# Lookup layer of an eight-layer token kernel: the first pair sum of each tile waits for the tile's candidate sums

## The chip, the core and the metric

The kernel runs on one core of a Trainium2 chip. A core has five engines that run their own instruction streams in order: PE (TensorE, matrix products and transposes), DVE (VectorE), ACT (ScalarE), POOL (GpSimd) and SP (SyncE, which issues transfers here). They are ordered against each other by semaphores: an instruction waits until a counter has reached a value, and adds to a counter when it is done. The metric is the device time of one launch in microseconds (us). For the kernel before, three timed runs took 1604.61, 1605.89 and 1609.22 us; their median is 1605.89 us.

## The reference, cut to what matters

The program takes 2048 tokens (8 x 256) of width 128 through four attention layers and four feed-forward layers in turn. The change lies in the second feed-forward layer, a lookup in a table by product keys:

```python
q = (xn @ w_q.T).reshape(b, s, 2, NH, KD).transpose(2, 0, 1, 3, 4)
sim = jnp.einsum('pbnhd,hkpd->pbnhk', q, keys_p)          # 2 x 8 heads x 32 keys
scores, idx = jax.lax.top_k(sim, K)                       # the best 8 of 32, twice
all_scores = scores[0][..., :, None] + scores[1][..., None, :]
sc, pk = jax.lax.top_k(all_scores, K)                     # the best 8 of the 64 sums
...
hmid = jnp.einsum('bnd,bnhkd->bnhk', inputs, down[indices])
hmid = jax.nn.sigmoid(sc) * jax.nn.gelu(hmid, approximate=False)
return jnp.einsum('bnhk,bnhkd->bnd', hmid, up[indices])
```

For each token and each of 8 heads, two lists of 32 similarities are added pairwise (1024 sums). The eight largest sums name eight table rows, and each of these rows counts with the sigmoid of its sum.

## The kernel before

The whole layer works on tiles of 128 tokens, of which there are 16. Nothing is gathered: all 1024 pair sums of a head are formed, and those below the eighth best are masked to zero. One tile goes through the engines like this (the line numbers are those of the listing and of the profile):

- PE forms the similarities of the tile (L1653), and ACT copies them from PSUM to `sims` (tile `sb_OT`, L1730, semaphore `sims_ready`).
- POOL forms, head by head, the 1024 **pair sums** into a ring of four slots, `pairsum` (tile `sb_KM`, L1773, semaphore `sum_ready`). From the fifth sum of the layer on, a sum waits until its slot has been read (`gated_ready`, L1771): sum 0 of a tile waits for head 4 of the tile before, sum 1 for head 5, and so on.
- DVE finds in the meantime the threshold of each head. **tops** takes 16 times the best 8 of 32 (L1805). **combine** adds the 20 pairs of these that can be among the best 8, in four tensor-tensor additions for all heads at once (L1812, from `sb_top` to `sb_QT`, semaphore `combos_done`, which grows by four a tile). **bests** takes the best 8 of the 20 for each head (L1822).
- ACT takes the sigmoid of each head's pair sums (L1748, into PSUM). Two PSUM halves take turns, so that the sigmoid of head h waits for head h-2 to be masked.
- DVE **masks** head by head (L1846): a sigmoid stays where the pair sum is at or above the eighth best, and becomes zero elsewhere. The result goes to `gated` (tile `sb_both`, semaphore `gated_ready`).
- PE turns each masked head and adds the eight heads up (L1677). DVE multiplies by the GELU of the products with the table (**mix**, L1831). PE multiplies with the second table (**upper**, L1667), and DVE adds the tile to the residual (**add**, L1836).
- PE forms the products with the first table for the next tile (**lower**, two halves, L1658), and ACT takes their GELU (L1738). ACT has to load another function table before the GELUs and again before the next sigmoid (rows ACT_TABLE_LOAD, of L1738 and L1748).

Heads 0 to 7 of a tile follow each other on DVE in one stream, and the work for the next tile is put between them by hand:

```python
        def step(first, last_, i, t):
            ...
            for h in range(PK_HEADS):
                ...                                   # mask head h (L1846)
                if h == 0 and first > 0:
                    mix(i - 1, t - 1)
                if h == 4:
                    if first > 0:
                        add_tile(i - 1)
                    if last_ > 0:
                        tops(i + 1, t + 1, 0, 16)
                        combine(i + 1, t + 1)
                if h == 5 and last_ > 0:
                    bests(i + 1, t + 1, 0, 4)
```

So the tops and the combine of tile i+1 stand on DVE between the masks of heads 4 and 5 of tile i. ACT's stream has the two GELUs of tile i+1 between the sigmoids of heads 6 and 7 of tile i. The first four tiles and the last four are written out; the eight between them run in a loop over four tiles (L1619 to L1629). Transfers play no part in this layer.

Of the kernel before, what the change touches and what calls it, by code (L numbers as in the profile page):

```python
# [1340 lines left out]
BANDS = ((0, 1, 8, 0), (1, 2, 4, 8), (2, 4, 2, 12), (4, 8, 1, 16))  # L1341
# [5 lines left out]
def feed_forward(nc, ctx, sb, sem, S, w):  # L1347
# [75 lines left out]
    top_done, combos_done, best_done = sem("top_done"), sem("combos_done"), sem("best_done")  # L1423
# [195 lines left out]
    def steps1(eng, step):  # L1619


        far = TILES
        for t in range(TPG):
            step(t, far, t, t)
        with eng.Fori(1, GROUPS - 1) as g:
            for t in range(TPG):
                step(far, far, TPG * g + t, t)
        for t in range(TPG):
            step(far, TPG - 1 - t, TILES - TPG + t, t)  # L1629
# [134 lines left out]
    def pool1(pool, A):  # L1764
        def step(first, last_, i, t):

            pool.wait_ge(sims_ready, i + 1)
            s = sims[:, t % 4, :].rearrange("p (h q k) -> p h q k", h=PK_HEADS, q=2)
            for h in range(PK_HEADS):
                if first > 0 or h >= 4:  # L1770
                    pool.wait_ge(gated_ready, PK_HEADS * i + h - 3)  # L1771
                dst = pairsum[:, h % 4, :].rearrange("p (i j) -> p i j", i=NK)
                pool.tensor_tensor(dst, s[:, h, 0, :].unsqueeze(2).broadcast_to([P, NK, NK]),  # L1773
                                   s[:, h, 1, :].unsqueeze(1).broadcast_to([P, NK, NK]), ALU.add)\
                    .then_inc(sum_ready, 1)

        steps1(pool, step)
# [616 lines left out]
```

## Time and profile before

| what | value |
|---|---|
| median of three timed runs | 1605.89 us (1604.61 to 1609.22) |
| the profiled execution's own time | 1600.34 us |
| its span, from the first to the last instruction | 1598.5 us |
| busy in the span: PE, DVE, ACT, POOL | 1406.6, 1023.4, 909.5, 706.3 us |
| mean granted clock of TensorE | 0.956 |
| the layer of the change, in the span | from 544 to 819 us, 275 us |
| POOL's 128 pair sums (L1773) | 240.2 us busy, 1912 ns each |
| DVE's 128 masks (L1846) | 158.4 us busy, 1274 ns each |
| ACT's 128 sigmoids (L1748) | 129.6 us busy, 1023 ns each |

Times in the rows are microseconds from the start of the span. A busy share over the whole span says little about this layer: PE is the busiest engine of the program, but the layer has its own order of work, and POOL, DVE and ACT hand it to each other tile by tile. It is read from the timeline of one tile, and then from how the tiles differ. Durations of POOL's instructions are rough in a profile; the distance between two starts is the better measure of one sum.

### The profile page before, as it was taken

How to read it: one execution, taken by the hardware profiler on the slowest of the kernel's cores; microseconds unless marked ns; L12 is line 12 of the kernel's file. 1: busy time of each engine (PE TensorE's matmuls, PEld its weight loads, DVE VectorE, ACT ScalarE, POOL GpSimd, SP SyncE). 2: the span in 40 equal slices, each digit the busy share in tenths (PEclk: the TensorE clock that was granted, in tenths of full speed). 3: DMA queues.
4: the chain of work that ended last, by engine and by line, in shares of the span. 5: the costliest groups of instructions: out<-in, count | busy, mean ns of one | idle time of the engine just before them, and what ended most of it. 6: DMA issues, size and time to landing. Idle time of an engine off the chain costs nothing.

```text
span 1598.5 us, 30106 instructions
## 1 busy us (share of the span) xinstructions
PE 1406.6 (88%) x9483; PEld 945.5 (59%) x9497; DVE 1023.4 (64%) x3372; ACT 909.5 (57%) x1883; POOL 706.3 (44%) x1068
## 2 busy tenths in 40 slices
PE   5997789999998577887778987799899999998998
PEld 2544357777776466776754553444477777775543
DVE  5663467666775799999965553443476666765444
ACT  3665356666665477777746664423376666664321
POOL 5341144554453589989854330100164444542300
PEclk9999799999999599999899999799999999998999
DMA  2007000000000000000000000000000000000000
GB/s 68 18 21 287 1 5 7 3 3 3 3 3 1 27 1 1 1 0 0 1 1 1 1 1 1 27 1 0 3 5 4 3 3 3 3 1 1 1 14 13
DMA packets 12666, 21.78 MB, mean 14 GB/s; under 512 B 3088, under 2 KB 9120, under 8 KB 11936
## 3 DMA queue, kind: packets, MB, share of 16 engines
q1 hardware_dynamic: 12576, 20.63, 3.7%
q8 instruction: 50, 0.82, 0.2%
q14 instruction: 40, 0.33, 0.1%
HBM read 19.58 MB, written 1.05 MB: 13 GB/s over the span
## 4 chain that ended last, share of the span: by engine, by line
PE 68%; DVE 15%; ACT 9%; issue 6%; POOL 1%; DVEq 0%; DMA 0%; ACTq 0%; SPq 0%; POOLq 0%
PE bank L934 7%; PE bank L969 7%; PE bank L947 6%; DVE sb_both L1846 4%; PE bank L900 4%; PE bank L921 4%; PE bank L1879 3%; PE bank L2118 3%; PE bank L901 3%; PE bank L913 3%; PE bank L409 2%; PE bank L451 2%; ACT sb_KM L598 2%; ACT sb_both L598 2%; ACT bank L1748 2%
## 5 line engine op out<-in xcount | busy, mean ns | idle before, releaser
L1213 POOL TENSOR_TENSOR sb_both<-sb_both,sb_winv 128x512 f32<-128x512 f32 x256 | 260.9, 1040 | 292.4 <-DVE sb_winv L1143 292.4
L1036 ACT ACTIVATE sb_both<-sb_both,sb_wneg 128x256 f32<-128x256 f32 x512 | 253.0, 495 | 126.8 <-DVE sb_wneg L1137 126.8
L1773 POOL TENSOR_TENSOR sb_KM<-sb_OT 128x1024 f32<-128x1024 f32 x128 | 240.2, 1912 | 31.9 <-DVE sb_both L1846 27.9
L1677 PE MATMUL bank<-sb_ident,sb_both 128*128 128x128 f32 x1024 | 139.2, 286 | 60.8 <-DVE sb_both L1846 38.6
L1137 DVE CUSTOM_DVE_ANT_0 sb_both<-bank,sb_pen 128x256 f32<-128x256 f32 x512 | 182.1, 420 | 0.0
L1296 POOL TENSOR_TENSOR sb_ntmp<-sb_rstd 128x2 f32<-128x2 f32 (+2 forms) x123 | 24.1, 196 | 338.5 <-DVE sb_rstd L218 332.1
L1846 DVE SCALAR_TENSOR_TENSOR sb_both<-sb_KM,sb_best,bank 128x1024 f32<-128x1024 f32 x128 | 158.4, 1274 | 10.6 <-ACT bank L1748 10.4
L1677 PEld LDWEIGHTS bank<-sb_ident,sb_both 128*128 128x128 f32 x1024 | 118.8, 147 | 75.3 <-DVE sb_both L1846 48.9
L1748 ACT ACTIVATE bank<-sb_KM 128x1024 f32<-128x1024 f32 x128 | 129.6, 1023 | 36.4 <-DVE sb_both L1846 31.9
L947 PE MATMUL bank<-sb_ident,sb_both 128*128 128x128 f32 x1024 | 134.1, 273 | 8.7 <-DVE sb_QT L1150 5.9
L947 PEld LDWEIGHTS bank<-sb_ident,sb_both 128*128 128x128 f32 x1024 | 118.3, 141 | 27.2 <-issue 12.7
L934 PE MATMUL bank<-sb_KM 64*128 64x256 f32 x1024 | 127.8, 389 | 0.0
L969 PE MATMUL bank<-sb_QT,sb_VP 128*64 128x256 f32 x1024 | 124.6, 385 | 3.2 <-DVE sb_QT L1150 1.6
L1150 DVE COPY sb_QT<-bank 128x512 f32<-128x512 f32 x128 | 88.0, 687 | 39.8 <-PE bank L947 39.0
L934 PEld LDWEIGHTS bank<-sb_KM 64*128 64x128 f32 x1024 | 93.5, 186 | 19.3 <-issue 7.7
L969 PEld LDWEIGHTS bank<-sb_QT,sb_VP 128*64 128x64 f32 x1024 | 68.6, 136 | 50.9 <-issue 21.9
L1036 ACT ACTIVATION_READ_ACCUMULATOR sb_both<-sb_both,sb_wneg 128x1 f32 x512 | 95.8, 187 | 0.0
L1046 ACT ACTIVATE sb_QT<-bank 128x512 f32<-128x512 f32 x128 | 75.1, 587 | 29.2 <-PE bank L947 29.2
L692 DVE TENSOR_REDUCE sb_VP<-bank 128x4 f32<-128x1024 f32 (+1 forms) x48 | 58.7, 1224 | 37.0 <-PE bank L415 36.8
L583 ACT ACTIVATE sb_xnT_all<-bank 128x1024 f32<-128x1024 f32 x48 | 49.0, 1022 | 52.7 <-PE bank L415 52.7
L1027 ACT ACTIVATE sb_KM<-bank 128x512 f32<-128x512 f32 x64 | 38.2, 597 | 58.2 <-PE bank L901 58.1
L1107 DVE COPY sb_KM<-bank 128x512 f32<-128x512 f32 x64 | 44.1, 690 | 39.8 <-PE bank L901 39.8
(282 smaller groups left out, 2769.3 us busy)
## 6 DMA issues: line engine op xcount, KB each, us to landing
sb_ctxT_in<-in_ctxT SPq DMA_DIRECT2D x24, 128.0 KB, 2.3
sb_F<-in_F SPq DMA_DIRECT2D x2, 1024.0 KB
sb_XO<-in_ctx SPq DMA_DIRECT2D x8, 128.0 KB, 2.0
sb_WKQ<-in_WKQ SPq DMA_DIRECT2D x1, 1024.0 KB, 9.0
sb_W1ALL<-in_ctxT SPq DMA_DIRECT2D x1, 1024.0 KB, 4.9
sb_xn_all<-in_keymask SPq DMA_DIRECT2D x1, 1024.0 KB, 4.5
out_x<-sb_x SPq DMA_DIRECT2D x4, 256.0 KB, 2.3
sb_x<-in_x SPq DMA_DIRECT2D x1, 896.0 KB, 5.0
```

Source lines behind the costliest of these rows:

```text
L934: last = pe.matmul(s[:, h, i, :], QK[rows, t, 0, i * P:(i + 1) * P], QK[rows, t, 1, :], start=True, stop=True)
L947: last = pe.transpose(bank[4 + i][:, n * P:(n + 1) * P], PRW[:, t % 4, h, i, kt * P:(kt + 1) * P], ident[:])
L969: last = pe.matmul(bank[6][rows, (t % 2) * SEQ:(t % 2 + 1) * SEQ], VW[:, kt, (2 * t + h) * 64:(2 * t + h + 1) * 64], PTW[:, t % 2, h, kt, ...
L1036: last = act.activation(p, p, ACT.Exp, scale=-1.0, bias=wneg[:, t % 4, h, i:i + 1], accum_out=wsum[:, t % 4, h, i:i + 1])
L1046: act.activation(PTW[:, t % 2, :, :, P:2 * P], bank[5][:].rearrange("p (h i q) -> p h i q", h=2, i=TPB), ACT.Copy).then_inc(w_pt[1], 1)
L1137: dve.tensor_tensor_reduce(PRW[:, t % 4, h, i, :], s[:, h, i, :], mask, -1.0, BIG, ALU.add, ALU.min, wneg[:, t % 4, h, i:i + 1]).then_inc( ...
L1150: dve.tensor_copy(PTW[:, t % 2, :, :, 0:P], bank[4][:].rearrange("p (h i q) -> p h i q", h=2, i=TPB))\
L1213: pool.tensor_tensor(p, p, winv[:, t % 4, :, i:i + 1].broadcast_to([P, 2, SEQ]), ALU.mult).then_inc(w_norm, 1)
L1677: last = pe.matmul(weight_bank(c), gated[:, h % 4, c * P:(c + 1) * P], ident[:], is_transpose=True, start=(h == 0 and c % 4 == 0), stop=(h ...
L1748: act.activation(sig_bank(h), pairsum[:, h % 4, :], ACT.Sigmoid).then_inc(sig_ready, 1)
L1773: pool.tensor_tensor(dst, s[:, h, 0, :].unsqueeze(2).broadcast_to([P, NK, NK]), s[:, h, 1, :].unsqueeze(1).broadcast_to([P, NK, NK]), ALU. ...
L1846: dve.scalar_tensor_tensor(out=gated[:, h % 4, :], in0=pairsum[:, h % 4, :], scalar=best[:, t % 2, h, TOPK - 1:TOPK], in1=sig_bank(h), op0 ...
```

## The change

One wait is added. Before the first pair sum of tile i, POOL now waits as well until the four additions of the combine of the same tile are done (`combos_done` at 4 (i + 1)):

```diff
         def step(first, last_, i, t):
 
             pool.wait_ge(sims_ready, i + 1)
+            pool.wait_ge(combos_done, len(BANDS) * (i + 1))
             s = sims[:, t % 4, :].rearrange("p (h q k) -> p h q k", h=PK_HEADS, q=2)
             for h in range(PK_HEADS):
                 if first > 0 or h >= 4:
```

No instruction that computes is added, removed or moved. The lines behind it move down by one. On POOL, the first four tiles of the layer stood like this before, with the semaphores that each row waits for:

```order
L1773 TENSOR_TENSOR sb_KM<-sb_OT 128x1024 [waits sims_ready]
L1773 TENSOR_TENSOR sb_KM<-sb_OT 128x1024 x3
L1773 TENSOR_TENSOR sb_KM<-sb_OT 128x1024 [waits gated_ready] x4
L1773 TENSOR_TENSOR sb_KM<-sb_OT 128x1024 [waits gated_ready,sims_ready]
L1773 TENSOR_TENSOR sb_KM<-sb_OT 128x1024 [waits gated_ready] x7
```

Now the same rows, at the head of the layer, and behind them the first rows of the loop:

```order
L1774 TENSOR_TENSOR sb_KM<-sb_OT 128x1024 [waits combos_done,sims_ready]
L1774 TENSOR_TENSOR sb_KM<-sb_OT 128x1024 x3
L1774 TENSOR_TENSOR sb_KM<-sb_OT 128x1024 [waits gated_ready] x4
L1774 TENSOR_TENSOR sb_KM<-sb_OT 128x1024 [waits gated_ready,combos_done,sims_ready]
L1774 TENSOR_TENSOR sb_KM<-sb_OT 128x1024 [waits gated_ready] x7
...
L1768 REGISTER_ALU [waits sims_ready]
L1772 ISA [waits combos_done]
L1774 TENSOR_TENSOR sb_KM<-sb_OT 128x1024 [waits gated_ready]
```

Of eight sums the first has the new wait, and in the loop its value is worked out in a register by one more small instruction of POOL's sequencer (L1768). What signals the wait stands on DVE, in this order, which is the same before and after (a stretch of one tile, from the mask of head 4 to that of head 6):

```order
L1846 SCALAR_TENSOR_TENSOR sb_both<-sb_KM,sb_best,bank 128x1024 [waits wT_done,sig_ready] x4
L1836 TENSOR_TENSOR sb_x<-bank,sb_x 128x128 [waits back_done1]
L208 MEMSET sb_scratch 128x1 [waits sims_ready]
L1805 MAX sb_top<-sb_OT 128x8 x16
L1812 TENSOR_TENSOR sb_QT<-sb_top 128x8x8 [waits top_done]
L1812 TENSOR_TENSOR sb_QT<-sb_top 128x8x4 x3
L1846 SCALAR_TENSOR_TENSOR sb_both<-sb_KM,sb_best,bank 128x1024 [waits wT_done,sig_ready]
L208 MEMSET sb_scratch 128x1 [waits combos_done]
L1822 MAX sb_best<-sb_QT 128x8 x4
L1846 SCALAR_TENSOR_TENSOR sb_both<-sb_KM,sb_best,bank 128x1024 [waits wT_done,sig_ready]
```

Nothing moved here. The sum that used to wait for the last of the four masks at the top (head 4) now waits for the fourth of the additions behind them.

## Rows read from the trace of the kernel before

**Rows 1.** Stages by window: each engine's busy us (instructions), then clock; three tiles.

```profile
636.09:652.62 16.53, 12.30 (x98) 10.88 (x98) 15.82 (x42) 12.50 (x14) 15.01 (x9) 1.00 0.00 0
685.94:702.59 16.65, 13.75 (x98) 12.02 (x98) 15.14 (x43) 12.60 (x14) 14.99 (x9) 0.90 0.00 0
768.84:786.34 17.50, 15.18 (x98) 13.53 (x98) 14.40 (x42) 12.31 (x13) 15.10 (x9) 0.75 0.00 1
```

**Rows 2.** Timeline of POOL: start, length, instructions, in brackets the idle time before.

```profile
544.39 7.50 POOL L1773 TENSOR_TENSOR sb_KM<-sb_OT 128x1024 f32<-128x1024 f32 x4 [4.01 <-ACT sb_OT L1730]
555.35 9.40 POOL L1773 TENSOR_TENSOR sb_KM<-sb_OT 128x1024 f32<-128x1024 f32 x5 [3.46 <-DVE sb_both L1846]
...
582.93 15.01 POOL L1773 TENSOR_TENSOR sb_KM<-sb_OT 128x1024 f32<-128x1024 f32 x8 [1.66 <-DVE sb_both L1846]
...
632.53 15.01 POOL L1773 TENSOR_TENSOR sb_KM<-sb_OT 128x1024 f32<-128x1024 f32 x8 [1.52 <-DVE sb_both L1846]
649.06 15.00 POOL L1773 TENSOR_TENSOR sb_KM<-sb_OT 128x1024 f32<-128x1024 f32 x8 [1.52 <-DVE sb_both L1846]
...
799.28 13.13 POOL L1773 TENSOR_TENSOR sb_KM<-sb_OT 128x1024 f32<-128x1024 f32 x7 [1.52 <-DVE sb_both L1846]
```

**Rows 3.** What ended POOL's idle time before the pair sums: us, times.

```profile
  DVE sb_both L1846: 27.9, 17
```

**Rows 4.** Timeline, one tile: POOL's sums 7 and 0, DVE's four additions, masks.

```profile
643.76 1.91 POOL L1773 TENSOR_TENSOR sb_KM<-sb_OT 128x1024 f32<-128x1024 f32 x1
645.62 1.92 POOL L1773 TENSOR_TENSOR sb_KM<-sb_OT 128x1024 f32<-128x1024 f32 x1
...
631.18 1.27 DVE L1846 SCALAR_TENSOR_TENSOR sb_both<-sb_KM,sb_best,bank 128x1024 f32<-128x1024 f32 x1
...
645.31 0.44 DVE L1812 TENSOR_TENSOR sb_QT<-sb_top 128x64 f32<-128x64 f32 x1
645.67 1.92 DVE L1812 TENSOR_TENSOR sb_QT<-sb_top 128x32 f32<-128x32 f32 x1
647.51 0.18 DVE L1812 TENSOR_TENSOR sb_QT<-sb_top 128x32 f32<-128x32 f32 x1
647.62 0.18 DVE L1812 TENSOR_TENSOR sb_QT<-sb_top 128x32 f32<-128x32 f32 x1
647.72 1.27 DVE L1846 SCALAR_TENSOR_TENSOR sb_both<-sb_KM,sb_best,bank 128x1024 f32<-128x1024 f32 x1
```

**Rows 5.** Additions of the first tile (544 to 553 us): ns min/median/max, starts.

```profile
L1812 DVE TENSOR_TENSOR sb_QT<-sb_top x4: 409/1924/1946, 546.0 to 550.0; 128x32 f32<-128x32 f32 x3, 128x64 f32<-128x64 f32 x1
```

**Rows 6.** All masks: ns min/median/max, first and last start.

```profile
L1846 DVE SCALAR_TENSOR_TENSOR sb_both<-sb_KM,sb_best,bank x128: 1257/1275/1282, 554.0 to 813.5; 128x1024 f32<-128x1024 f32 x128
```

**Rows 7.** Timeline of ACT: table loads and GELUs around head 7, five places.

```profile
563.38 1.08 ACT L1738 ACTIVATE sb_xn_all<-bank 128x512 f32<-128x512 f32 x2
566.27 1.28 ACT L1748 ACT_TABLE_LOAD   x1 [1.81 <-DVE sb_both L1846]
...
646.17 1.09 ACT L1738 ACTIVATE sb_xn_all<-bank 128x512 f32<-128x512 f32 x2
649.06 1.28 ACT L1748 ACT_TABLE_LOAD   x1 [1.81 <-DVE sb_both L1846]
...
663.95 0.60 ACT L1738 ACTIVATE sb_xn_all<-bank 128x512 f32<-128x512 f32 x1 [0.52 <-PE bank L1658]
...
682.38 1.28 ACT L1748 ACT_TABLE_LOAD   x1 [0.97 <-DVE sb_both L1846]
...
697.63 0.60 ACT L1738 ACTIVATE sb_xn_all<-bank 128x512 f32<-128x512 f32 x1 [0.82 <-PE bank L1658]
```

**Rows 8.** The tile of 17.50 us: its first addition, second GELU and table load.

```profile
780.47 0.67 DVE L1812 TENSOR_TENSOR sb_QT<-sb_top 128x64 f32<-128x64 f32 x1
...
782.17 0.60 ACT L1738 ACTIVATE sb_xn_all<-bank 128x512 f32<-128x512 f32 x1 [1.17 <-PE bank L1658]
782.79 1.28 ACT L1748 ACT_TABLE_LOAD   x1
```

**Rows 9.** The layer's last sigmoid, and the sum it waited for.

```profile
812.45 1.03 ACT L1748 ACTIVATE bank<-sb_KM 128x1024 f32<-128x1024 f32 x1 [0.84 <-POOL sb_KM L1773]
```

## The prediction, made before the changed kernel ran

> **What bounds the kernel now.** I read the layer's tiles as windows first, then POOL's timeline through them, then one tile instruction by instruction, and last the same places in tiles that differ.
>
> The windows [rows 1] show that a tile takes 16.53 us at full granted clock (1.00, that is 2.4 GHz throughout), 16.65 us where part of it ran at 1.2 GHz (mean 0.90), and 17.50 us in one tile (mean 0.75). POOL is busy for about 15 us of each, DVE for 14.4 to 15.8. POOL's timeline [rows 2] shows why this matters: eight pair sums run back to back, and then POOL idles once a tile. There are fifteen such gaps, nine of 1.52 us and six of 1.66 us, 23.6 us together; masks ended 27.9 us of idle time on POOL in all [rows 3]. A row of eight starts with sum 1 of a tile and ends with sum 0 of the next.
>
> The single tile [rows 4] shows what the gap consists of. The first addition of the combine starts at 645.31, while sum 7 runs (643.76 to 645.67), and takes 0.44 us. The second starts at 645.67 and takes 1.92 us, as long as sum 0, which started at 645.62. The third and fourth take 0.18 us each. So an addition with two SBUF inputs doesn't run beside a pair sum: it waits for the sum's end. At the head of the layer, where four sums run back to back, three of the four additions take 1.9 us [rows 5]. The chain of one tile is therefore: sum 0 ends, additions 2 to 4 end, mask 5 runs (647.72, 1.27 us), and sum 1 starts at 649.06 [rows 2, 4]. So sum 0 holds up what sum 1 waits for.
>
> Starts of sums lie 1.87 us apart ((645.62 - 632.53) / 7 [rows 2, 4]), so eight take 14.96 us, and 14.96 + 1.57 (from 647.49, where the next could start, to 649.06) gives the 16.53 us.
>
> **The change, part by part.** It adds one wait a tile, 16 in all, and moves no instruction. Queued behind it on POOL are only the sums of the same tile; who waits for these is ACT (sigmoids) and, behind it, DVE.
>
> *The additions.* With sum 0 held, addition 2 still starts at 645.67, when sum 7 ends. The others follow at the distance that rows 4 show for a free port, 0.10 us (647.51, 647.62, 647.72): 645.77, 645.88, and mask 5 at 645.98 in place of 647.72, 1.74 us earlier. The combine ends at 645.88 + 0.18 = 646.06.
>
> *Sum 0.* From the end of mask 5 (648.99) to the start of sum 1 take 0.08 us. With the same step sum 0 starts at 646.14. In the loop POOL's sequencer has one more register instruction, which no row prices; nothing at one end, another step of 0.08 us at the other, and I take 0.05. Sum 0 at 646.19 is 0.57 us later than before.
>
> *Sum 1.* It follows at 646.19 + 1.87 = 648.06, 1.00 us earlier than before. Mask 5, for which it used to wait, has ended by 645.98 + 1.27 = 647.25. So POOL's own loop becomes 14.96 + 0.57 = 15.53 us.
>
> *Whether the others keep up.* DVE's loop, from mask 5 (631.18) to the next first addition (645.31), takes 14.13 us [rows 4], and with a free port 0.4 more to the next mask 5: 14.5 us. So DVE has room, and the first addition will wait longer than now for sum 7, about a microsecond. ACT's loop goes from the table load behind mask 5 to the end of the second GELU. At full clock that is 14.73 us: the load one period before 649.06 lies at 632.53, and the GELUs end at 646.17 + 1.09 = 647.26 [rows 7]. In tiles with a dip of the clock the second GELU waits for PE: 664.55 - 649.06 = 15.49 us, and 698.23 - 682.38 = 15.85 us [rows 7]. Those tiles go from 16.65 to between 15.53 and 15.87, a gain of 0.78 to 1.12; I take 0.9. The sums from 1 on lie later behind mask 5 than before (2.08 against 1.34 us), and through the sigmoid of head 6 the GELUs move with them: their end lies 3.5 us behind the start of sum 7 (647.26 - 643.76), so 13.1 + 3.5 = 16.6 us behind sum 0, and mask 5 of the next round ends at 15.53 + 1.06 = 16.6 us. The two are level; that is why ACT is the next limit.
>
> *The slow tile.* In the tile of 17.50 us the first addition already waited only 0.67 us, and the table load followed the second GELU (ended at 782.77, load at 782.79) [rows 8]. PE set its length; I count no gain.
>
> *Both ends.* At the head, sum 0 of the first tile is held by some 2 us, but the first sigmoid starts only behind the GELUs and a table load; the additions end about 5 us earlier (546.5 against 551.9 [rows 5]) and mask 0 doesn't start before 554.0 [rows 6]. That hides it. In the first tile, sum 7 ended at 562.88 (564.75 - 1.87 [rows 2]), so mask 5 would end near 564.5, level with the GELUs (564.46), and the load moves from 566.27 to 564.6: 1.7 us gained [rows 7]. At the tail, the last sigmoid waits for its sum (812.45 [rows 9]), and the sums lie 0.74 us later behind the masks: 0.7 us lost.
>
> **Sum:** 8 tiles x 1.0 + 5 x 0.9 + 0 + 1.7 - 0.7 = 13.5 us gained. Against the profiled execution: 1600.34 - 13.5 = 1586.8. The median of the timed runs lies 5.55 us above that execution, so the median becomes 1605.89 - 13.5 = 1592.4 us. Bounds within this case: 14 tiles at 15.48 us (no extra register step, no dip of the clock) give 14 x 1.1 + 1.0 = 16.4 us, 1589.5; the smallest gain in the dipped tiles gives 12.9 us, 1593.0.
>
> **A rule to weigh.** The masks read an SBUF tensor, a scalar per row from SBUF, and PSUM. If that scalar made them wait for POOL as the additions do, the change would only move the collision: sum 0 and mask 5 now start together. The masks take 1257 to 1282 ns over all 128, though POOL's sums ran beside most of them [rows 6, 2], so they don't wait. The Trainium skill, "SBUF — State Buffer", section "SBUF: two separate sides", says that VectorE and GpSimd share one port pair as an exclusive lock, taken for the whole instruction by whichever starts first, and that on VectorE's side instructions with two SBUF inputs count. By that rule read strictly, the scalar included, the gain would be about zero (the second rival below); read as tensors alone it gives the sum above, and the trace agrees with this reading, 0.44 and 1.92 us for additions beside sums and 1.27 us for masks.
>
> **The rivals.**
>
> *ACT becomes the bound.* If most tiles are like the worst dipped one (15.85 us), 13 tiles gain about 0.73 and the ends 1.0: 10.5 us, 1595.4. With three tiles like the 17.50 one it would be 8.3 us, 1597.6. For it: the two loops are level even at full clock. Against it: 8 of 14 tiles showed no dip.
>
> *The collision moves to mask 5, and nothing changes.* Mask 5 would start 0.16 us ahead of sum 0 and hold it up for 1.27 us; sum 0 would start near 647.3, and the loop would be 14.96 + 1.7 = 16.6 us. Time 1606. Against it stands the even length of the masks.
>
> *Slower: the granted clock stays at half.* The gaps of PE change with the new rhythm. A tile at half clock long enough takes 17.50 us, and there the new wait saves nothing. If all 13 went that way: 13 x 0.94 + 0.7, about 13 us more, 1619. It decides from about half of the tiles on, where 0.94 lost in one cancels 1.0 gained in another. Against it: a shorter tile leaves PE less idle, and the stage had one such tile in 15.
>
> **How the numbers follow.** Forecast 0.62; ACT as the bound 0.24; nothing changes 0.09; slower 0.05. A measurement of this kernel can tell about 0.3% (4.8 us) from no change. The first two lie beyond that, so faster 0.87, with a little of the second rival on either side; within 0.3% 0.08, slower 0.05. The range takes in the forecast's upper gain (1589.5) and the first rival (1597.6), each with some 3 us for the spread that the three runs show (1604.61 to 1609.22): 1586 to 1600.
>
> **What would show it.** In the profile after: the gap on POOL moves from before sum 1 to before sum 0, shrinks to about 0.5 us, and is ended by the additions (L1812) in place of a mask. In each tile only the first addition is long (about 1.0 to 1.4 us), the other three take 0.18 us. The tile takes 15.5 us, the layer some 262 us in place of 275. ACT's idle time ahead of the table load (1.81 us) nearly goes. The prediction is wrong if additions 2 to 4 stay long, if masks grow beyond 1.3 us, or if POOL idles over 1.5 us before sum 0 because DVE comes late to the combine.

## The result

The first four timed runs of the changed kernel gave 1578.69 to 1589.48 us, median 1584.11, against a median of 1605.25 for four runs of before: the ratio worked out from all of them is 0.9874, interval 0.9851 to 0.9897. Faster, as forecast, but 1.9 us below the range. Two later measurements of the same kernel, with more runs of before beside them, gave 1589.89 us (ratio 0.991, 0.9879 to 0.994) and 1586.92 us (0.9902, 0.9867 to 0.9937). All 16 runs together have a median of 1586.9 us; the 44 runs of before that stood beside them have 1604.06. The change is worth some 14 to 20 us of 1604; the forecast was 13.5.

First the layer. It runs from the first copy of similarities (L1730) to the last add to the residual. The rows give each stretch's length, then busy us (and instructions) of PE, PEld, DVE, ACT and POOL, the mean granted clock and DMA. Of the first trace of before, with what lies ahead of the layer and behind it:

```profile
0.00:543.72 543.72, 479.53 (x3572) 319.33 (x3572) 334.06 (x1235) 313.31 (x769) 234.09 (x487) 0.96 0.10 33
543.72:819.77 276.05, 212.56 (x1570) 187.01 (x1570) 255.46 (x666) 200.89 (x222) 240.93 (x132) 0.92 0.00 1
819.77:1598.50 778.73, 714.54 (x4342) 439.15 (x4356) 433.87 (x1472) 395.32 (x893) 231.30 (x450) 0.97 0.01 5
```

Of the first trace of after:

```profile
0.00:550.28 550.28, 485.43 (x3572) 320.65 (x3572) 333.99 (x1235) 313.53 (x769) 234.10 (x487) 0.95 0.09 33
550.28:810.20 259.92, 209.81 (x1570) 186.35 (x1570) 233.69 (x666) 201.59 (x222) 240.82 (x132) 0.93 0.00 1
810.20:1587.70 777.50, 712.74 (x4342) 438.37 (x4356) 433.62 (x1471) 395.25 (x893) 231.27 (x450) 0.97 0.01 5
```

The layer is 16.1 us shorter. DVE's busy time in it falls by 21.8 us with the same 666 instructions: that is the time that additions stood waiting and were counted as busy. POOL's busy time doesn't change.

POOL's timeline after, in the columns of [rows 2]:

```profile
553.20 7.50 POOL L1774 TENSOR_TENSOR sb_KM<-sb_OT 128x1024 f32<-128x1024 f32 x4 [6.26 <-DVE sb_QT L1813]
561.81 7.52 POOL L1774 TENSOR_TENSOR sb_KM<-sb_OT 128x1024 f32<-128x1024 f32 x4 [1.11 <-DVE sb_both L1847]
569.85 15.00 POOL L1774 TENSOR_TENSOR sb_KM<-sb_OT 128x1024 f32<-128x1024 f32 x8 [0.52 <-issue]
585.38 15.01 POOL L1774 TENSOR_TENSOR sb_KM<-sb_OT 128x1024 f32<-128x1024 f32 x8 [0.52 <-issue]
600.91 15.01 POOL L1774 TENSOR_TENSOR sb_KM<-sb_OT 128x1024 f32<-128x1024 f32 x8 [0.52 <-issue]
616.47 15.00 POOL L1774 TENSOR_TENSOR sb_KM<-sb_OT 128x1024 f32<-128x1024 f32 x8 [0.56 <-DVE sb_QT L1813]
632.34 15.00 POOL L1774 TENSOR_TENSOR sb_KM<-sb_OT 128x1024 f32<-128x1024 f32 x8 [0.86 <-DVE sb_QT L1813]
...
787.84 15.01 POOL L1774 TENSOR_TENSOR sb_KM<-sb_OT 128x1024 f32<-128x1024 f32 x8 [0.52 <-issue]
```

A row of eight is now one tile, sums 0 to 7. The gap stands ahead of sum 0, it is 0.52 to 0.56 us in most tiles, and the additions (L1813) end it where the profile names a releaser. The gap ahead of sum 1 is gone. From 569.85 to 787.84 are 14 tiles, 15.57 us each, against 16.53 and 16.65 us before (16.64 on average of 14, one slow tile among them).

One tile of after, POOL's sum 7 and sum 0 first, then DVE, as in [rows 4]; two additions that overlap stand in one row:

```profile
660.97 1.92 POOL L1774 TENSOR_TENSOR sb_KM<-sb_OT 128x1024 f32<-128x1024 f32 x1
663.44 1.91 POOL L1774 TENSOR_TENSOR sb_KM<-sb_OT 128x1024 f32<-128x1024 f32 x1 [0.55 <-DVE sb_QT L1813]
...
661.76 1.21 DVE L1813 TENSOR_TENSOR sb_QT<-sb_top 128x64 f32<-128x64 f32 x1
662.90 0.28 DVE L1813 TENSOR_TENSOR sb_QT<-sb_top 128x32 f32<-128x32 f32 x2
663.10 0.18 DVE L1813 TENSOR_TENSOR sb_QT<-sb_top 128x32 f32<-128x32 f32 x1
663.20 1.26 DVE L1847 SCALAR_TENSOR_TENSOR sb_both<-sb_KM,sb_best,bank 128x1024 f32<-128x1024 f32 x1
```

Only the first addition waits, for sum 7, which ends at 662.89. The other three follow 0.10 us apart, mask 5 starts at 663.20, and sum 0 0.16 us behind the end of the fourth addition (663.28). ACT around the same place, as in [rows 7]:

```profile
661.06 1.03 ACT L1748 ACTIVATE bank<-sb_KM 128x1024 f32<-128x1024 f32 x1 [0.84 <-POOL sb_KM L1774]
662.10 1.28 ACT L1738 ACT_TABLE_LOAD   x1
663.40 1.08 ACT L1738 ACTIVATE sb_xn_all<-bank 128x512 f32<-128x512 f32 x2
664.55 1.28 ACT L1748 ACT_TABLE_LOAD   x1
```

The idle 1.81 us ahead of the table load is gone: the GELUs end at 664.48, mask 5 at 664.46, level as reckoned. What ACT waits for now is POOL, ahead of the sigmoid of head 6 (0.84 us). Over the whole layer, what ended POOL's idle time, what the additions and what the masks took:

```profile
  DVE sb_QT L1813: 11.1, 9
  issue: 3.6, 7
  DVE sb_both L1847: 1.1, 1
...
L1813 DVE TENSOR_TENSOR sb_QT<-sb_top x64: 176/179/1262, 552.5 to 787.5; 128x32 f32<-128x32 f32 x48, 128x64 f32<-128x64 f32 x16
...
L1847 DVE SCALAR_TENSOR_TENSOR sb_both<-sb_KM,sb_best,bank x128: 1250/1274/1284, 560.5 to 803.9; 128x1024 f32<-128x1024 f32 x128
```

By the same view of both traces, POOL's idle time ahead of the sums falls from 31.9 to 15.8 us (the first two lines end 14.7 of it). No addition takes 1.9 us any more, and the masks are as long as in [rows 6].

### The profile page after: what moved, and what is told of

It is laid out like the page before. It is cut to its first block, busy times and chain, and to the rows that moved or that the text cites. A ratio compares the mean times of both kernels' runs of the same rounds, so it can differ in the third digit from the quotient of the medians.

```text
span 1587.7 us, 30115 instructions
## 1 busy us (share of the span) xinstructions
PE 1408.0 (89%) x9483; PEld 945.4 (60%) x9497; DVE 1001.3 (63%) x3372; ACT 910.4 (57%) x1883; POOL 706.2 (44%) x1068
## 4 chain that ended last, share of the span: by engine, by line
PE 68%; DVE 12%; ACT 9%; issue 5%; POOL 4%; DVEq 0%; DMA 0%; ACTq 0%; SPq 0%; POOLq 0%
PE bank L934 7%; PE bank L969 7%; PE bank L947 6%; PE bank L900 4%; PE bank L921 4%; PE bank L1880 3%; PE bank L2119 3%; PE bank L901 3%; POOL sb_KM L1774 3%; PE bank L913 3%; DVE sb_both L1847 3%; PE bank L409 3%; PE bank L451 2%; ACT sb_KM L598 2%; ACT sb_both L598 2%
## 5 line engine op out<-in xcount | busy, mean ns | idle before, releaser
L1774 POOL TENSOR_TENSOR sb_KM<-sb_OT 128x1024 f32<-128x1024 f32 x128 | 240.1, 1912 | 15.8 <-DVE sb_QT L1813 11.1
```

## The experiments

The first four set one theory against three rivals. Theory 1: the mechanism is the predicted one, the layer gives what its rows show, and the rest of the 20 us lies in the spread of single executions. The rivals: something outside the layer gains too, the first trace of before was unusual, or freeing the additions is the whole gain and POOL has room.

**The kernel before, again.** No edit.

> The kernel before, unchanged, for a second trace and for the spread of one kernel against itself. Theory 1 (the layer gives about 16 us, and the rest of the measured gain of 20 is the spread of single executions in layers that the change doesn't touch): ratio 1.000 within 0.002; the layer takes 275 to 276 us again, with tiles of 16.53 and 16.65 us, while the parts ahead of it and behind it move by several us against the first trace. Theory 2 (the first trace of before was a lucky one in the layer itself): the layer takes 278 to 280 us here, with several tiles near 17.5 us.

Median 1603.63 us over 12 runs, against 1603.97 us over 29 runs of before: ratio 0.9992 (0.9971 to 1.0013). Its trace, with the same three stretches:

```profile
0.00:550.32 550.32, 485.53 (x3572) 320.70 (x3572) 334.15 (x1235) 313.67 (x768) 234.95 (x487) 0.95 0.09 33
550.32:826.21 275.89, 212.96 (x1570) 186.85 (x1570) 256.64 (x666) 201.15 (x222) 241.03 (x132) 0.93 0.00 1
826.21:1607.80 781.59, 716.15 (x4342) 440.89 (x4356) 433.82 (x1471) 395.34 (x893) 232.01 (x450) 0.97 0.01 4
```

The layer takes 275.89 us, as in the first trace (276.05). But the stretch ahead of it is 6.6 us longer than in the first trace (550.32 against 543.72), and the one behind it 2.9 us (781.59 against 778.73), in code that is the same. Over the 29 runs of before that stood beside these experiments, single executions lie between 1594.32 and 1610.43 us. Theory 1 holds for before; its first trace was not unusual in the layer.

**The changed kernel, twice more.** No edit.

> The changed kernel, unchanged, for a second trace and a narrower interval. Theory 1 (the layer gives 16 us, the rest is spread): ratio near 0.990, that is 16 us; layer 259 to 261 us, tiles of 15.2 to 15.9 us. Theory 2 (something outside the layer gains as well): ratio 0.987 or lower again, and the parts ahead of the layer or behind it are shorter than in both traces of before.

> The changed kernel once more, unchanged. Theory 1 (the change is worth the 14 to 16 us that its layer loses; the 20 us of the first four runs are the spread of executions): ratio 0.989 to 0.992, layer 259 to 262 us. Rival (the true gain is 20 us and the second measurement of 14 was the odd one): ratio 0.987 or lower.

1589.89 us (ratio 0.991, 0.9879 to 0.994) and 1586.92 us (0.9902, 0.9867 to 0.9937). The layer in the two traces:

```profile
549.15:810.80 261.65, 208.58 (x1570) 184.51 (x1570) 235.02 (x666) 201.55 (x222) 242.00 (x138) 0.93 0.00 1
```

```profile
549.26:810.90 261.64, 208.34 (x1570) 184.43 (x1570) 235.24 (x666) 201.91 (x222) 241.97 (x138) 0.93 0.00 1
```

Three layers of after average 261.07 us, two of before 275.97: 14.9 us. Outside the layer the traces take 1322.5 and 1331.9 us (before), 1327.8, 1326.7 and 1323.2 us (after): no gain there that stands out of the spread. That goes with theory 1. The later two layers are 1.7 us longer than the first at their very end only (see the ends, below); the 14 tiles take 218.0 us, from 568.83 to 786.81 and from 568.94 to 787.01, as in the first. The intervals of the three measurements overlap (0.9879 to 0.9897, 16.5 to 19.4 us, is common to all), so whether the true value lies nearer to 15 or to 19 us isn't settled.

**The wait in half of the tiles.** Only the eight tiles of the loop wait.

```diff
-            pool.wait_ge(combos_done, len(BANDS) * (i + 1))
+            if first >= TILES and last_ >= TILES:
+                pool.wait_ge(combos_done, len(BANDS) * (i + 1))
```

> The new wait only in the eight tiles of the loop, not in the four tiles in front and the four behind. If each wait frees the additions of its own tile (theory 1), eight of 16 waits give about half: tiles whose additions are held free take 15.5 to 15.9 us, the others 16.5, and 8 x 1.0 = 8 us are gained, ratio 0.995. If the gain comes from elsewhere, it doesn't go with the count of the waits.

1594.91 us over 12 runs, ratio 0.996 (0.9941 to 0.9978), the layer 268.4 us in its trace: 7.5 us less than before. POOL's timeline in the layer:

```profile
582.85 14.99 POOL L1775 TENSOR_TENSOR sb_KM<-sb_OT 128x1024 f32<-128x1024 f32 x8 [1.66 <-DVE sb_both L1848]
599.51 13.13 POOL L1775 TENSOR_TENSOR sb_KM<-sb_OT 128x1024 f32<-128x1024 f32 x7 [1.66 <-DVE sb_both L1848]
613.20 15.01 POOL L1775 TENSOR_TENSOR sb_KM<-sb_OT 128x1024 f32<-128x1024 f32 x8 [0.56 <-DVE sb_QT L1814]
...
722.11 16.86 POOL L1775 TENSOR_TENSOR sb_KM<-sb_OT 128x1024 f32<-128x1024 f32 x9 [0.55 <-DVE sb_QT L1814]
740.49 15.00 POOL L1775 TENSOR_TENSOR sb_KM<-sb_OT 128x1024 f32<-128x1024 f32 x8 [1.52 <-DVE sb_both L1848]
```

The gap changes its place and size with the first tile that waits and changes back with the first that doesn't, at 740.49. Within the loop a tile takes 15.56 us ((722.11 - 613.20) / 7). The gain goes with the count of the waits.

**Sum 0 later still.** It waits for the mask of head 5, which stands behind the additions on DVE.

```diff
-            pool.wait_ge(combos_done, len(BANDS) * (i + 1))
+            if first > 0:
+                pool.wait_ge(gated_ready, PK_HEADS * i - 2)
```

> In place of the wait for the candidate sums, sum 0 of a tile waits for the mask of head 5 of the tile before, which stands behind the additions on DVE. The additions stay free of sum 0 as in the changed kernel, but sum 0 starts some 1.2 us later. Theory 1 (POOL's eight sums and the gap ahead of sum 0 make the tile): 14.96 us and a gap of 1.7 us, 16.6 to 16.7 us a tile, so about the time of before, ratio 1.000 to 1.003, although no addition waits for POOL beyond sum 7. Rival (freeing the additions is the whole gain, and POOL has room): tiles of 15.5 us stay, ratio 0.99.

1603.44 us, ratio 0.9994 (0.9974 to 1.0014): the gain is gone, though only the first addition of each tile is long (at most 1.58 us; the other three take 0.18, from the second tile on). POOL's timeline:

```profile
621.28 15.00 POOL L1775 TENSOR_TENSOR sb_KM<-sb_OT 128x1024 f32<-128x1024 f32 x8 [1.74 <-DVE sb_both L1848]
638.02 14.99 POOL L1775 TENSOR_TENSOR sb_KM<-sb_OT 128x1024 f32<-128x1024 f32 x8 [1.74 <-DVE sb_both L1848]
```

A tile takes 16.74 us, eight sums and a gap of 1.7. So freeing the additions is not by itself the gain. What counts is the gap on POOL, wherever it stands; the rival falls.

**Sum 0 a little earlier.** If that is so, a smaller gap should give more. The wait is for the second addition of the tile.

```diff
-            pool.wait_ge(combos_done, len(BANDS) * (i + 1))
+            pool.wait_ge(combos_done, len(BANDS) * i + 2)
```

> The wait is for the second of the four additions of a tile in place of the fourth. Additions stand 0.10 us apart, and from an addition's end to the sum pass about 0.13 us, so the fourth addition should have the port before sum 0 asks for it. Theory 1 (POOL's eight sums and the gap ahead of sum 0 make the tile): the gap shrinks from 0.57 to about 0.37 us, tiles from 15.5 to 15.3, the layer by some 3 us to about 257 us; ratio 0.988 to 0.990. Rival A (ACT makes the tile): layer as in the changed kernel, 260 us. Rival B (sum 0 takes the port ahead of the third or fourth addition): one addition of 1.9 us in each tile, tiles of 16.5 us, ratio near 1.

1579.48 us, ratio 0.9856 (0.982 to 0.9892), the layer 257.2 us in its trace, 3.9 us below the average of after (2.7 of it in the 14 tiles, the rest at the layer's end). POOL's timeline, and what its additions took:

```profile
568.41 15.00 POOL L1774 TENSOR_TENSOR sb_KM<-sb_OT 128x1024 f32<-128x1024 f32 x8 [0.32 <-issue]
583.73 15.01 POOL L1774 TENSOR_TENSOR sb_KM<-sb_OT 128x1024 f32<-128x1024 f32 x8 [0.32 <-issue]
...
783.76 15.01 POOL L1774 TENSOR_TENSOR sb_KM<-sb_OT 128x1024 f32<-128x1024 f32 x8 [0.32 <-issue]
...
L1813 DVE TENSOR_TENSOR sb_QT<-sb_top x64: 177/180/1267, 551.2 to 783.7; 128x32 f32<-128x32 f32 x48, 128x64 f32<-128x64 f32 x16
```

The gap is 0.2 us smaller, the two additions behind the released wait take 0.18 us as before, and 14 tiles take 15.38 us each. Neither rival holds: the layer is shorter than the changed kernel's, and no addition takes 1.9 us. This is the fastest version of the study, ahead of both kernels by its layer; by the timed runs its interval overlaps with that of after.

**Two wider additions.** Fewer instructions stand in the gap, at the price of 28 candidates in place of 20.

```diff
-BANDS = ((0, 1, 8, 0), (1, 2, 4, 8), (2, 4, 2, 12), (4, 8, 1, 16))
-CANDIDATES = 20
+BANDS = ((0, 2, 8, 0), (2, 8, 2, 16))
+CANDIDATES = 28
```

> The candidate sums are formed by two wider additions (128 and 96 elements a row, 28 candidates a head in place of 20) with the changed kernel's wait for all of them. Theory 1: two distances of 0.1 us less, the wider additions some 0.1 us more, so the gap ahead of sum 0 is 0.4 to 0.5 us, tiles 15.4 us, layer 258 to 260 us; ratio 0.989 to 0.991. DVE's bests of 28 in place of 20 cost some 0.06 us a tile, on an engine that waits anyway. Rival (ACT makes the tile): 260 us, no difference.

1586.86 us, ratio 0.9892 (0.9858 to 0.9927), layer 260.1 us. The gap is 0.45 to 0.49 us in most tiles, as expected, but a gain of 1 to 2 us can't be told from after. With the wait for the first of the two alone:

> Two wider additions, and sum 0 waits for the first alone. Theory 1: the gap ahead of sum 0 is about 0.3 us, tiles 15.25 us, layer 256 to 257 us, ratio 0.986 to 0.989, the shortest of the four. Rival A (ACT makes the tile): 260 us. Rival B (sum 0 takes the port ahead of the second addition): the second addition takes 1.9 us, tiles of 16.5 us.

1584.31 us, ratio 0.9877 (0.9842 to 0.9911), layer 258.4 us. The gap is 0.28 to 0.32 us in most tiles and a tile 15.35 us, hardly less than with the second of four additions; the layer is not the shortest, as had been expected, but 1.2 us longer. The sums aren't the reason: behind the last mask this trace takes 7.88 us, that of the second addition 6.25, because its last matrix products (L1667) ran at a granted clock of 0.53. The trace of the two bands shows what happens when DVE comes late to the combine, in a tile whose clock fell:

```profile
565.48 15.00 POOL L1774 TENSOR_TENSOR sb_KM<-sb_OT 128x1024 f32<-128x1024 f32 x8 [0.45 <-issue]
582.02 15.01 POOL L1774 TENSOR_TENSOR sb_KM<-sb_OT 128x1024 f32<-128x1024 f32 x8 [1.54 <-issue]
597.48 15.00 POOL L1774 TENSOR_TENSOR sb_KM<-sb_OT 128x1024 f32<-128x1024 f32 x8 [0.45 <-issue]
```

One gap of 1.54 us, and the tile behind it is back at 15.46 us.

## Why the prediction was right, and where it was wrong

The mechanism was the predicted one; what failed are sizes. In the sum it is the term of the tiles in which the clock falls, 5 x 0.9 + 0 = 4.5 us, in whose place the first trace shows 7.3. In the range it is the 3 us for the spread, in whose place executions of one kernel lie 16 us apart.

**The chain of one tile: right.** It was put as sum 7, additions, sum 0, with mask 5 beside sum 0, from [rows 4]. Reckoned were a gap of 0.57 us ahead of sum 0 (measured from the distance of starts: 0.56 to 0.68, once 0.90), additions 2 to 4 at 0.18 us (they are), a POOL loop of 15.53 us (15.57), and a first addition that waits longer than before for sum 7 (0.30 to 1.26 us with its own time, where 1.0 to 1.4 was reckoned: behind most tiles whose clock fell DVE comes later and waits less). The extra step on POOL was taken at 0.05 us between 0 and 0.08; from the end of the fourth addition to sum 0 pass 0.16 us in the tile shown, of which 0.08 is the ordinary step, so the upper end holds there. The later wait and the earlier one show that the gap is paid for one to one: 1.74 us gives 16.74 us a tile, 0.55 gives 15.56, 0.32 gives 15.32 (starts 568.41 and 583.73).

**The ends: right in the first trace.** The first tile gained 1.75 us (1.7 reckoned: 15.84 to 14.09 us between its first mask and the next tile's). The tail lost 0.7 us: from the first to the last mask of the last tile pass 11.41 us, 10.69 before. The head cost nothing: from the first copy of similarities to mask 0 pass 10.2 us, 10.3 before. What the sum had no term for is the last matrix products of the layer (L1667), on which the last add waits. Their windows in the first and the second trace of after:

```profile
807.85:809.87 2.02, 2.02 (x17) 1.90 (x17) 1.12 (x9) 0.00 (x0) 0.51 (x3) 1.00 0.03 8
806.82:810.47 3.65, 3.65 (x17) 3.42 (x17) 1.12 (x9) 0.00 (x0) 1.68 (x9) 0.53 0.02 4
```

In the second trace, and likewise in the third (3.55 us, clock 0.55), they run at 1.2 GHz for most of the stretch, and the layer ends 1.5 to 1.6 us later. In neither trace of before did they; whether the changed rhythm brings this about is not shown.

**The dipped tiles and the slow tile: the term of the sum that was mis-sized.** For five tiles in which the clock falls I took 0.9 us, because ACT's loop gave up to 15.85 us, and for the slow tile nothing. Four tiles in a row of after, by their first masks, with the clock as the third column from the end:

```profile
574.54:590.37 15.83, 13.50 (x98) 12.03 (x98) 14.16 (x42) 12.75 (x14) 15.31 (x9) 0.89 0.00 0
590.37:605.60 15.23, 12.23 (x98) 10.88 (x98) 14.62 (x42) 12.50 (x14) 14.71 (x9) 1.00 0.01 2
605.60:621.43 15.83, 13.51 (x98) 12.03 (x98) 14.16 (x43) 12.69 (x14) 15.27 (x9) 0.89 0.00 1
621.43:636.69 15.26, 12.25 (x98) 10.88 (x98) 14.56 (x43) 12.50 (x14) 14.40 (x9) 1.00 0.01 2
```

The dipped tile does take 15.83 us. But the next takes 15.23, because the loop through DVE and ACT is faster than POOL's at full clock and makes up what it lost. The sums go on at 15.53 us meanwhile (569.85, 585.38, 600.91 in POOL's timeline). Two of the 14 gaps grew, to 0.86 and 0.64 us, but not by late additions. Ahead of the sum at 632.34 the last addition stands like this:

```profile
631.69 0.18 DVE L1813 TENSOR_TENSOR sb_QT<-sb_top 128x32 f32<-128x32 f32 x1
```

It ended at 631.87, and POOL took 0.47 us to start in place of 0.13 to 0.17. Both gaps stand at the same two tiles of the loop in all three traces of after, also behind a tile at full clock; their cause is open. I had added up the longer of two loops tile by tile, where a late tile costs only what POOL itself has to wait. POOL's loop also set the tiles of 16.65 us before. In one of them (sum 0, and the first addition of the same tile):

```profile
678.80 1.92 POOL L1773 TENSOR_TENSOR sb_KM<-sb_OT 128x1024 f32<-128x1024 f32 x1
...
679.22 1.58 DVE L1812 TENSOR_TENSOR sb_QT<-sb_top 128x64 f32<-128x64 f32 x1
```

DVE comes only after sum 0 has started, so the first addition waits to its end, and three additions in place of two stand behind it: the gap there is 1.66 us in place of 1.52. Over 14 tiles the gain is 15.0 us in place of the reckoned 12.5 in this trace: at 15.57 us each, the eight at full clock give 7.7 (8.0 reckoned), the five dipped ones 5.4 (4.5), and the slow one 1.9 (0). The layer's gain was 16.1 us here and 14.9 on average of the traces, against 13.5.

**The slow tile.** It is the largest part of the miss. No trace of after had a tile of 17.5 us; both traces of before have one (17.50 and 17.22 us). So the 1.9 us were gained because no such tile came, and whether that is the change or the chance of the clock is open. With two bands one tile took 17.1 us, with POOL's gap at 1.54 us, and the tile behind it 14.9 us. The run with the later wait has one too, here with the tile behind it:

```profile
691.71:708.84 17.13, 14.80 (x98) 13.30 (x98) 14.07 (x42) 12.84 (x14) 15.39 (x10) 0.80 0.00 0
708.84:725.18 16.34, 12.48 (x98) 10.90 (x98) 15.30 (x43) 12.73 (x14) 14.60 (x8) 1.00 0.00 0
```

The two take 33.47 us, twice 16.74, and POOL's sums keep their distance (688.23, 704.97, 721.70). That supports the same reading; for the changed kernel itself no trace shows it. The upper bound left the slow tile out as well: by [rows 1] 14 tiles of 15.48 us give 17.3 us in place of 16.4.

**The range: the second error, and the one that put the measured time outside.** I took some 3 us for the spread, from three runs of before (1604.61 to 1609.22). The profiled execution, 1600.34 us, which the prediction used as well, already lay 4.3 us below the lowest of them. Executions of one kernel lie 16 us apart (1594.32 to 1610.43), and a median of four to six moves by several us: 1584.11, 1589.89 and 1586.92 us for the same kernel. The last two lie inside the range. With the 16.1 us of the first trace in place of 13.5 the forecast would have been 1589.8 us, still inside; the 5.7 us from there to 1584.11 the layer's rows don't show, so that the first median fell outside is in part chance. The forecast was also put against a median of 1605.89 us where 29 runs give 1603.97, so it lay 1.9 us too high from the start. Of the 5.5 us between the forecast (1592.4) and the median of all 16 runs (1586.9), 1.9 are this, 1.4 the layer (14.9 less 13.5: 2.5 more in the tiles, 1.1 less at the ends), and some 2 us remain open; they are smaller than the spread outside the layer.

**The rivals.** ACT as the bound: it is level with POOL at full clock and behind it in dipped tiles, but not the bound over several tiles: with a smaller gap the tiles went on to 15.38 us. The collision moving to mask 5: the masks take 1250 to 1284 ns beside sum 0, so they don't wait for the port, and of the two readings of the Trainium skill's rule ("SBUF — State Buffer", section "SBUF: two separate sides") the one that counts tensors alone agrees with these traces. Clock at half: the mean granted clock in the layer is 0.93, against 0.92 and 0.93 before (and a slow tile costs 17.50 - 16.58 = 0.92 us by [rows 1], not 0.94, which changes nothing).

## What to carry to other kernels

Where a short instruction of one engine doesn't run beside a long one of another, as an addition of 0.18 us beside a sum of 1.9 us here, and the long ones stand back to back, the short one can lose up to a whole long one; holding the long queue with a semaphore until the short ones are through can cost less than it saves (a gap of 0.55 us in place of 1.52 to 1.66). Find the engine whose loop closes the period, and count only what is added to that loop: a wait that is off it may grow, as the first addition's did, and a late tile of another engine can be made up for by the next, if that engine's loop is the faster one. Before a range is set for a change of one per cent, look at how far single executions of the same kernel lie apart, and not at three of them.

## What the runs showed of the hardware that had not been expected

The same code ahead of the layer took 543.7 us in one execution and 550.3 in another, with granted clocks of 0.96 and 0.95, and that difference is nearly half as large as the change. From the end of the signalling instruction to the start of the sum pass 0.16 us with the added wait (663.28 to 663.44), against 0.08 us with one wait (648.99 to 649.06 before). The register instruction explains about a third of the difference, since in the tiles that are written out, where there is none, the step is 0.13 us and the gap 0.52 us, against 0.55 in the loop. The rest may be the second wait ahead of the same instruction; that was not taken apart further.
